# One 128-node block per turn of an edge-attention stage, in place of two 64-node half-blocks

## The reference, cut to what matters

```python
h = (x @ W.T).reshape(n, H, D)                     # H = 8 heads of D = 32
alpha = einsum('ehd,hd->eh', h[src], a_src) + einsum('ehd,hd->eh', h[dst], a_dst)
enc = relu(edge_attr @ edge_W.T + edge_b).reshape(-1, H, D)
alpha = alpha + sum(enc * h[dst], axis=-1)
alpha = where(alpha >= 0, alpha, 0.2 * alpha)
amax = segment_max(alpha, dst, n)
ex = exp(alpha - amax[dst])
denom = segment_sum(ex, dst, n)
attn = ex / maximum(denom[dst], 1e-10)
out = segment_sum(h[src] * attn[..., None], dst, n) + bias
x = x + out + linear_attention(layernorm(x))
x = x + experts(layernorm(x))
```

## Time and profile before

| | us |
|---|---|
| median of three runs | 4003.45 |
| span of the profiled execution | 4846.5 |
| VectorE busy in it | 2700.2 (56%) |
| TensorE busy in it | 4087.7 (84%) |
| ScalarE busy in it | 2291.3 (47%) |
| GpSimd busy in it | 1780.1 (37%) |

### The profile page before, as it was taken

How to read it: one execution, slowest core, us unless ns; L and a number is a source line. 1 busy time by engine, 2 the same in 40 slices (tenths; PEclk the granted TensorE clock), 3 DMA queues, 4 the chain that set the end, 5 groups by cost and what they waited for, 6 DMA issues and landing times. The chain is left out here.

```text
span 4846.5 us, 80424 instructions
## 1 busy us (share of the span) xinstructions
PE 4087.7 (84%) x22764; PEld 1897.1 (39%) x22765; DVE 2700.2 (56%) x5470; ACT 2291.3 (47%) x6074; POOL 1780.1 (37%) x1859
## 2 busy tenths in 40 slices
PE   5699988957888887788887878878887999999999
PEld 3333322312333333333333333333333666666666
DVE  7566723336666666676666666667666333333333
ACT  4444445524555555555555555555554433333332
POOL 3255555644454445444444444445440000000000
PEclk8799989976888888888888887888887799999999
DMA  7555556655555555555555555555552100000000
GB/s 216 160 165 162 164 177 201 210 156 154 161 168 165 158 165 164 162 168 168 159 162 152 163 157 161 162 159 168 164 162 67 61 8 1 8 8 8 8 8 8
DMA packets 378173, 629.74 MB, mean 130 GB/s; under 512 B 83912, under 2 KB 245063, under 8 KB 377536
## 3 DMA queue, kind: packets, MB, share of 16 engines
q1 hardware_dynamic: 277266, 356.80, 23.4%
q0 software_dynamic: 93408, 257.23, 19.5%
q10 hardware_dynamic: 7104, 11.01, 0.7%
HBM read 520.59 MB, written 104.12 MB: 129 GB/s over the span
## 5 line engine op out<-in xcount | busy, mean ns | idle before, releaser
L1629 POOL DMA_INDIRECT s_rows<-scratch_src_rows,s_idx_w x1312 | 1257.6, 959 | 1367.6 <-PE s_ps_a L1692 563.3
L1837 DVE SCALAR_TENSOR_TENSOR s_enc<-s_enc,s_a_dst,s_ps_d 128x512 f32<-128x512 f32 x904 | 634.9, 741 | 313.3 <-DMA p_feats<-in_edge_f,p_tcol_i 160.8
L1734 ACT ACTIVATE s_enc<-s_ps_f 128x1024 f32<-128x1024 f32 x452 | 459.5, 1017 | 516.6 <-remote 265.5
L1692 PE MATMUL s_ps_a<-s_rows,s_hot_e 128*64 128x264 f32 x3616 | 647.1, 490 | 44.9 <-DVE s_rows L1920 32.4
L2285 DVE SCALAR_TENSOR_TENSOR kx_y_all<-e_ps_o,kx_gate,kx_y_all 128x256 f32 (+1 forms) x392 | 173.5, 480 | 684.2 <-PE e_ps_o L2340 684.2
L1920 DVE TENSOR_TENSOR s_rows<-s_rows,s_ps_x 128x1024 f32<-128x1024 f32 x452 | 545.7, 1207 | 13.6 <-ACT s_a_w L1765 8.7
L1688 PE MATMUL s_ps_a<-ke_sums,k_ident 128*128 x790 | 341.0, 520 | 217.1 <-DVE ke_sums L1913 123.6
L1913 DVE TENSOR_TENSOR ke_sums<-s_ps_a,ke_sums 128x264 f32 x509 | 218.3, 429 | 505.3 <-remote 263.9
L1669 PE MATMUL s_ps_s<-s_enc,s_head_sum 128*32 128x256 f32 x3616 | 353.7, 469 | 152.9 <-DVE s_enc L1837 121.2
L1779 ACT ACTIVATE s_hot_e<-k_iota_row,s_rel_w 128x64 f32<-128x64 f32 x1808 | 480.5, 339 | 0.0
L1787 ACT COPY ke_sums<-s_ps_a 128x264 f32 x395 | 148.6, 376 | 552.5 <-remote 337.8
(11 more groups left out here) (280 smaller groups left out, 5259.0 us busy)
## 6 DMA issues: line engine op xcount, KB each, us to landing
s_table<-scratch_dst_parts SPq DMA_DIRECT2D x904, 96.0 KB
s_rows<-scratch_pre_rows SPq DMA_DIRECT2D x124, 528.0 KB
s_relb<-scratch_rel_rows SPq DMA_DIRECT2D x226, 256.0 KB
scratch_pre_rows<-n_rows SPq DMA_DIRECT2D x62, 528.0 KB
scratch_pre_rows<-m_rows SPq DMA_DIRECT2D x62, 528.0 KB
s_rows<-scratch_src_rows,s_idx_w POOLq DMA_INDIRECT x1312
s_feat<-scratch_step_parts SPq DMA_DIRECT2D x226, 54.0 KB
s_pen_w<-scratch_pen_rows SPq DMA_DIRECT2D x228, 48.1 KB
```

The lines of the kernel that those rows point to most:

```text
L1629: pool.indirect_dma_start(out=rows[:, d % R, m, :], out_offset=None, in_=scr["src_table"], in_offset=bass.IndirectOffsetOnAxis(ap=idx_w[:, ...
L1692: last = PE.matmul(ps_a[t * WN:(t + 1) * WN, sub, 0:SRC_W], hot_e[:, d % 3, 2 * sub + t, :], rows[:, d % R, 2 * sub + t, :], start=(sub == ...
L1734: A.activation(enc[:, d % 2], ps_f[:], ACT.Relu).then_inc(enc_made, 1)
L1837: V.scalar_tensor_tensor(out=enc[:, d % 2, c, :], in0=enc[:, d % 2, c, :], scalar=a_dst[:, c:c + 1], in1=ps_d[:, c, :], op0=ALU.add, op1=A ...
```

## The change

A block is 128 nodes instead of 64 (`WN = P`), there are 49 instead of 98, and a turn of 512 edges has one block for both its steps. The number of turns stays: T is 806 steps both times, before D = ceil((806 + 97) / 4) * 2 = 452, now D = ceil((403 + 48) / 2) * 2 = 452. `spread_out` becomes six matmuls of 128 rows x 512 edges, `aggregate` four matmuls of 128 columns that accumulate in one of two PSUM banks, without identity, put back or `value_load`; `reduce` stays behind it. VectorE does the one addition. SyncE loads the block's table in one DMA behind one `value_load`. The one-hots are 128 wide, `sums` has half its size, the experts' weights get room of their own and are loaded from the beginning of the combine stage, which has no band matmuls and divides and adds in SBUF.

```diff
-WN = P // 2
+WN = P
@@ stage_start
-                        for b in range(2):
-                            sp.dma_start(scr["dst_parts"][2 * d + b].rearrange("c n w -> n c w"), parts[b * WN:(b + 1) * WN, d % RP]).then_inc(d_stored[d % RP], 16)
+                        sp.dma_start(scr["dst_parts"][d], parts[:, d % RP].rearrange("p c w -> p (c w)")).then_inc(d_stored[d % RP], 16)
@@ plan_dims
-    NJ = 2 * NT
-    T = -(-E // GE)
-    D = -(-(T + NJ - 1) // 4) * 2
+    NJ = NT
+    T = 2 * -(-E // (2 * GE))
+    D = -(-(T // 2 + NJ - 1) // 2) * 2
@@ stage_edges, SyncE, load(d)
-                    for sub in range(2):
-                        i = KS + 2 * k + sub
-                        j = sp.value_load(turns_w[0:1, w % 4, i:i + 1], min_val=0, max_val=NJ - 1)
-                        if sub == 0:
-                            wait(sp, spread[1], d - RL + 1)
-                        sp.dma_start(table[:, u, sub, :], row(scr["dst_parts"], j).rearrange("o c n w -> (o c n) w")).then_inc(table_in[u], 16)
+                    j = sp.value_load(turns_w[0:1, w % 4, k:k + 1], min_val=0, max_val=NJ - 1)
+                    wait(sp, spread[1], d - RL + 1)
+                    sp.dma_start(table[:, u].rearrange("p a w -> p (a w)"), row(scr["dst_parts"], j).rearrange("o n w -> (o n) w")).then_inc(table_in[u], 16)
@@ stage_edges, TensorE, spread_out(d)
-                    for sub in range(2):
-                        for c in range(2):
-                            PE.matmul(ps_d[:, c, sub * GE:(sub + 1) * GE], table[c * 64:(c + 1) * 64, u, sub, C:HALF],
-                                      hot[c * 64:(c + 1) * 64, v, sub * GE:(sub + 1) * GE], start=(sub == 0), stop=False, skip_group_check=True)
-                    for c in range(2):
-                        for sub in range(2):
-                            last = PE.matmul(ps_d[:, c, sub * GE:(sub + 1) * GE], table[:, u, sub, c * P:(c + 1) * P],
-                                             hot[:, v, sub * GE:(sub + 1) * GE], start=False, stop=True, skip_group_check=True)
-                        last.then_inc(spread[c], 1)
+                        PE.matmul(ps_d[:, c, :], table[:, u, c, C:HALF], hot[:, v, :], start=True, stop=False)
+                        PE.matmul(ps_d[:, c, :], table[:, u, 1, c * P:(c + 1) * P], hot[:, v, :], start=False, stop=False)
+                        PE.matmul(ps_d[:, c, :], table[:, u, 0, c * P:(c + 1) * P], hot[:, v, :], start=False, stop=True).then_inc(spread[c], 1)
@@ stage_edges, TensorE, aggregate(d)
-                    if k > 0:
-                        j = pe.value_load(turns_w[0:1, w % 4, KS + 2 * k:KS + 2 * k + 1], min_val=0, max_val=NJ - 1)
...
-                    wait(pe, added, 2 * d)
-                    if k > 0:
-                        PE.matmul(ps_a[:, 0, 0:SRC_W], keep["ident"][:], sums[:, bass.ds(j, 1), :].rearrange("p o w -> p (o w)"),
-                                  start=True, stop=False, skip_group_check=True)
-                    for sub in range(2):
-                        for t in range(TG):
-                            last = PE.matmul(ps_a[t * WN:(t + 1) * WN, sub, 0:SRC_W], hot_e[:, d % 3, 2 * sub + t, :], rows[:, d % R, 2 * sub + t, :],
-                                             start=(sub == 1 or k == 0), stop=True, skip_group_check=True)
-                        last.then_inc(summed[sub], 1)
+                    wait(pe, added, d - 1)
+                    for m in range(TD):
+                        last = PE.matmul(ps_a[:, d % 2, 0:SRC_W], hot_e[:, d % 3, m, :], rows[:, d % R, m, :], start=(m == 0), stop=(m == TD - 1))
+                    last.then_inc(summed, 1)
@@ stage_edges, ScalarE
-                        A.activation(hot_e[:, d % 3, m, :], keep["iota_row"][:, 0:WN], ACT.Abs, bias=...)
+                        A.activation(hot_e[:, d % 3, m, :], keep["iota_row"][:], ACT.Abs, bias=...)
-                def put_back(d):
...
-                    A.copy(sums[:, bass.ds(j, 1), :].rearrange("p o w -> p (o w)"), ps_a[:, 0, 0:SRC_W]).then_inc(added, 1)
@@ stage_combine
-                for u in range(R):
-                    sp.wait_ge(banded[u], len(range(u, NT, R)))
                 for e in range(EXPERTS):
                     for m, n in enumerate(("W1", "W2", "Wo")):
                         sp.dma_start(keep["weights"][:, m, e], ins[n][:, e]).then_inc(experts_in, 16)
+                sp.wait_ge(x1_made, NT)
...
-                        for b in range(2):
-                            last = PE.matmul(ps_n[u][b * WN:(b + 1) * WN, 0:SRC_W], band_sum[:], sums[:, 2 * i + b, :], start=True, stop=True)
-                        last.then_inc(banded[u], 1)
```

More of the change, by code:

```diff
@@ L450, in _ @@
                 pe.wait_ge(past_made, 1)
-                for b in range(SB):
-                    PE.matmul(ps_jc[0:SP, b:b + 1], past.rearrange("j (p b) -> j b p", b=SB)[:, b, :], ones[0:NJ, 0:1], start=True, stop=True)
-                for u in range(2):
-                    last = PE.matmul(ps_j[u], ones[0:NJ, :], past[:, u * SH:(u + 1) * SH], start=True, stop=True)
-                last.then_inc(j_done, 1)
+                for b in range(QB):
+                    PE.matmul(ps_jc[0:SP, b:b + 1], past.rearrange("j (p b) -> j b p", b=QB)[:, b, :], ones[0:NJ, 0:1], start=True, stop=True)
+                PE.matmul(ps_j, ones[0:NJ, :], past, start=True, stop=True).then_inc(j_done, 1)
                 pe.wait_ge(fold_in, 16 * 4)
@@ L1567, in load_turns @@
                 def load_turns(w):
-                    wait(sp, added, KS * (w - 3))
+                    wait(sp, added, KW * (w - 3))
                     sp.dma_start(turns_w[:, w % 4, :], scr["turns"][w:w + 1, :]).then_inc(turns_in[w % 4], 16)
@@ L1625, in _ @@
                         continue
-                    wait(pool, summed[1], d - R + 1)
+                    wait(pool, summed, d - R + 1)
                     wait(pool, enc_made, d - 4)
```

218 lines of the change are left out of this document (92 added, 126 removed).

## The result

The changed kernel is slower: 4126.47 us (median of four runs, 4125.31 to 4130.61) against 4002.65 for before, a ratio of 1.0327 with a 95% interval of 1.0304 to 1.0349.

What follows compares the result with a forecast made beforehand. The timed edge stage was taken as bound by TensorE and VectorE at once. Other stages 2173.5 - s - 38 plus an edge stage of 2208 gave 4343 - s, about 4280 us with s = 60; range 4140 to 4415.

Steps and rivals of the forecast that it cites:

- s: Stages outside edges: their share of the 843 us by which the profile exceeded the unprofiled run; 60, bounds 0 and 150.
- stalls: Edge stage after: a factor of 1.025 on 452 turns of 4.68 us, bounds 1.00 to 1.06.
- The start stage: Start stage: one store per block less was to change the time by 0.
- Combine: Combine stage: VectorE starts earlier without band matmuls, and the experts' weights are there by its end; -38 us, bounds -15 and -50.
- TensorE's chain: Edge stage: TensorE's own work per turn, 3.82 us before and 4.68 after the change.
- rival D: Edge stage: fp32 weights not hidden, `aggregate` 2.57 us, total 4575, or TensorE's clock partly at half; chance 0.08.
- change of block: TensorE in the edge stage: about 0.10 us at each switch between blocks of matmuls, six per turn becoming four.
- The tail: Edge stage's end: twelve aggregations no longer wait for the sum before them; 30 us for 12, -20.
- A: Edge stage: less than counted, s near 150 and free block changes outside the profile; 4050 to 4150 us, chance 0.07.
- B: Edge stage: SyncE's table loads bound the timed run too, and half go; faster, some 3830 us, chance 0.04.
- C: Edge stage: no change, only pure columns count, 4.18 us per turn; 4004 us, chance 0.04.
- low end: Whole kernel: the range's lower limit, 4140 us, with no stalls and s = 150.

Runs made afterwards that it cites:

- e0: The kernel before, without an edit, run and profiled a second time; 3999.59 us.
- e6: The kernel after with half of `weigh` left out on VectorE; 4123.27 us.
- e2: The kernel after with its start stage's table store split into two DMAs of 64 nodes; 4143.1 us, ratio 1.0349.
- e8b: The kernel after with the experts' weights asked for only at the end of the combine stage; 4127.19 us.
- e7: The kernel before with one table load and one `value_load` per turn, used for both steps; 4001.75 us, ratio 0.9992.
- e15b: The kernel before with half of `weigh` and half of `multiply` left out on VectorE; 3924.38 us, ratio 0.9805.
- e18: e15b with the window's loads moved to later turns; 3857.61 us, ratio 0.9664 to before.
- e1: The kernel before with one start-stage store per 128 nodes and the table in memory as block, node, half; 5140.91 us, ratio 1.2835.
- e14: The kernel before, second table store issued by ScalarE, router weights waited for late, on the slower chip; 4770.83 us, ratio 0.9959.
- e14b: The same kernel as e14, on a chip where before takes about 4000 us; 3978.72 us, ratio 0.9953.
- e8: The same edit of the kernel after as e8b, on the slower chip; 4867.3 us, ratio 1.0092.
- e15: The same edit of the kernel before as e15b, on the slower chip; 4737.69 us, ratio 0.9886.

## Why the prediction was wrong in size

- **"The other stages give up s of the 843 ...; I take s = 60".** This is the step that failed. The first profile was 843 us longer than the runs, and the prediction put nearly all of it into the edge stage. Measured, s is 147 (e0). That takes 87 us off the forecast, and it makes the turn before 4.23 and not 3.91 to 4.0, so that the change costs 0.42 us per turn, not 0.7 to 0.8. The bounds given, 0 to 150, held it. The profile ahead of the prediction had the hint, since its kv (L1091) and mix (L1195) stages hold gathers too, and nothing said that those were spared:

```profile
L1195 POOL DMA_INDIRECT m_rows<-scratch_src_rows,m_idx x248 | 235.7, 951 | 174.7 <-issue 64.6 <-PE m_ps_n L1221 56.7 <-DMA kn_w_qkv<-in_w_qkv_t 33.8
L1091 POOL DMA_INDIRECT n_rows<-scratch_src_rows,n_idx x248 | 235.0, 947 | 207.0 <-PE n_ps_g L948 107.5 <-issue 62.7 <-DMA n_idx<-scratch_edge_idx 33.3
```

- **"times 1.025 for stalls".** None, -53 us. VectorE has 0.19 of its time free (busy for 1138 of 1400), and neither it nor a load holds TensorE between 1200 and 2600; e6 moves the time by 3 us.
- **"The start stage: one store per block less, 0".** It was -22 (e2: 16 of it come back with the second store; the other 6 stay open). SyncE's queue had not been looked at there.
- **Combine, -38.** It was -26. The part on the weights "asked for 35 us ahead of the end" was worth 0 (e8b).
- **TensorE's chain.** Right: 4.65 us for 4.68, 1.40 for 1.39, 1.98 for 1.94. That the total is closer than its parts is luck (4.48 + 0.17 for 4.43 + 0.25). The eight records of `aggregate` take 1.98 us and not the 2.57 of rival D, which falls. The change of block costs 0.09 to 0.10 us as read from the earlier trace rows: L1638 to L1627 is 0.31, where the same shape follows itself in 0.22. The Trainium skill (TensorEngine Tiling (Array Packing), Key Properties) has a drain at each change of tiling mode. The rows are consistent with it, at 0.1 us for the change from 128 rows to 30, but no run sets a drain apart from another cost of the change.
- **The tail.** The stage ends 39 us after the last turn's first `multiply`, 52 us in before: -13 for -20.

The sum: 4283 - 87 (s) - 53 (stalls) - 17 (451 turns of 4.652) + 11 (head and tail) - 22 (start) + 12 (combine) - 2 (the rest) is 4125, the span of the profile after.

Of the rivals, A (4050 to 4150, chance 0.07) had the place and half of the mechanism: s near 150 was right, free changes of block were not, so that its number is in part luck. B falls with e7, C and D with the trace after. The low end, 4140, was built from s = 150 and no stalls, which is what happened. The 22 us of the start stage took the time below it, with 6 us of the edge stage; the 12 us that the combine stage fell short by and 1 us of the rest went the other way.

## What to carry to other kernels

Where a profile is far longer than the timed runs, compare every stage that uses the same resource before the difference is given to one of them; the timed kernel can be bound by another engine than the profile shows. Half-width matmuls side by side in the array cost about half of what full-width ones do here (1.04 us for 1.98), so widening them to save bookkeeping beside them pays only if the bookkeeping is the longer part. And a bound can have another close behind it: e15b and e18 took VectorE away and found a queue of loads.

## What was not expected of the hardware

**A load whose source starts with a dimension of 2 kept about two packets in flight.** In e1 the loads bring the same 96 KB in the same pieces of 768 bytes. In the second profile of before the packets of that size in flight at one time, taken every 0.1 us from 1200 to 2600, are 4.8 on average where there is any, and up to 18; in e1 they are 1.9, most often exactly 2 and never above 4. The turn goes from 4.23 to 6.81 us, and the bandwidth falls:

```profile
1200.00:2600.00 1400.00, 1052.80 (x6069) 414.02 (x6062) 797.37 (x1519) 673.29 (x1953) 569.28 (x596) 0.76 0.46 137
```

SyncE is held as well (start, us, what):

```profile
1600.05 7.23 SPq L1599 DMA_DIRECT2D s_table<-scratch_dst_parts  x4
...
1611.87 3.54 SPq L1599 DMA_DIRECT2D s_table<-scratch_dst_parts  x2
```

The Trainium skill (DMA: Bandwidth & Descriptors, Why a DMA increments its semaphore by 16 and not by 1) states that the slowest dimension of both access patterns sets the number of engines, the largest up to 16 that divides both. The source here starts with a dimension of 2, the two halves, so it would be 2, and the count of packets in flight agrees. That this slowed the loads is argued and not shown: no run here separates it from the longer issue on SyncE.

**One chip of five was slower, and in three stages only.** On it kv, mix and edges took 28%, 15% and 34% longer than on another (e14 beside e14b: 407.6 to 319.6, 414.8 to 360.6, 2632.6 to 1963.5), and start, combine and experts did not; e8 and e15 beside e8b and e15b give 28% to 36% for kv and edges and 13% for mix. Both the ratio of the change (1.009 there for e8, 1.032 elsewhere) and what TensorE waits for in the edge stage depend on it. The cause is open.
